# A three-layer graph attention kernel: places of DVE's checks, chain and statistics, and the load of x in two parts

## The reference

```python
def gat_layer(x, src, dst, W, a_src, a_dst, b, n_nodes):
    h = x @ W
    e = leaky_relu((h @ a_src)[src] + (h @ a_dst)[dst], 0.2)
    m = segment_max(e, dst)
    ex = exp(e - m[dst])
    alpha = ex / segment_sum(ex, dst)[dst]
    return segment_sum(alpha[:, None] * h[src], dst) + b

h = maximum(layernorm(x), 0)
x = x + gat_layer(relu(gat_layer(h, W1 128x256)), W2 256x128)
h = maximum(layernorm(x), 0)
x = x + gat_layer(h, W 128x128)
```

## Time and profile before

| | us |
|---|---|
| median of 3 runs | 685.88 (685.61 to 686.31) |
| profiled execution | 684.96 |
| its span in the trace | 683.1 |
| DVE busy | 639.8 (94%) |
| PE busy | 591.5 (87%) |
| ACT busy | 484.3 (71%) |
| POOL busy | 460.1 (67%) |
| mean granted clock of PE, as a share of full | 0.963 |

### The profile page before, as it was taken

One profiled execution on the slowest core, in us unless ns is written; L12 is line 12 of the kernel. 1 busy time (PEld: TensorE's weight loads), 2 busy tenths in 40 slices (PEclk: granted clock), 3 DMA queues, 4 the chain that ended last, 5 costly groups with the idle time before them and its releaser, 6 DMA issues.

```text
span 683.1 us, 13824 instructions
## 1 busy us (share of the span) xinstructions
PE 591.5 (87%) x5571; PEld 573.1 (84%) x5571; DVE 639.8 (94%) x911; ACT 484.3 (71%) x719; POOL 460.1 (67%) x448
## 2 busy tenths in 40 slices
PE   1729865899978999999999899999989989999994
PEld 1628755789878999899989799999988979999994
DVE  3999999999999989999987998999998899999993
ACT  0416544656969688887666788989886698888891
POOL 5579101889928565775954675858598678697883
PEclk9978986899999999999999999999999999999999
DMA  2410002000000000000100100000010010110001
GB/s 70 119 56 2 1 7 6 35 2 1 20 1 1 20 1 20 2 1 8 26 14 1 27 1 20 2 19 1 8 20 20 1 27 6 35 32 8 20 1 42
DMA packets 22325, 12.07 MB, mean 18 GB/s; under 512 B 12393, under 2 KB 20055, under 8 KB 22255
## 3 DMA queue, kind: packets, MB, share of 16 engines
q1 hardware_dynamic: 21455, 9.85, 6.3%
q0 software_dynamic: 800, 1.26, 0.6%
HBM read 9.47 MB, written 1.64 MB: 16 GB/s over the span
## 4 chain that ended last, share of the span: by engine, by line
DVE 51%; PE 29%; issue 8%; DMA 5%; POOL 4%; ACT 2%; POOLq 0%; DVEq 0%
PE ps L1813 21%; DVE scratch L951 20%; DVE ps L1067 15%; DVE scratch L1149 5%; DMA xr<-in_x 3%; POOL scratch L751 2%; DVE ps L1069 2%; DVE ps L1079 1%; PE ps L1866 1%; PE ps L1821 1%; PE ps L1844 1%; DVE scratch L1067 1%; DMA gathered<-in_edges,start_i 1%; DVE gathered L1149 1%; PE ps L1780 1%
## 5 line engine op out<-in xcount | busy, mean ns | idle before, releaser
L1813 PE MATMUL ps<-hB,scratch 125*125 125x129 f32 x3450 | 404.5, 276 | 21.1 <-DVE scratch L1149 17.6
L1813 PEld LDWEIGHTS ps<-hB,scratch 125*125 125x125 f32 x3450 | 390.9, 189 | 28.4 <-DVE scratch L1149 22.6
L751 POOL TENSOR_TENSOR scratch<-scratch,C 125x625 f32<-125x625 f32 x239 | 304.3, 1285 | 113.0 <-ACT scratch L1569 110.9
L1067 DVE SCALAR_TENSOR_TENSOR ps<-C,a_unit,ps 125x625 f32<-125x625 fp8e3 x330 | 275.4, 866 | 2.3
L1567 ACT ACTIVATE scratch<-gathered,r_neg 125x625 f32<-125x625 f32 x219 | 176.6, 806 | 20.3 <-PE ps L1813 19.2
L1569 ACT ACTIVATE scratch<-scratch,r_src 125x625 f32<-125x625 f32 x219 | 178.9, 817 | 7.1
L1452 ACT ACTIVATE C<-ps 125x1000 fp8e3<-125x1000 f32 x80 | 78.2, 1001 | 77.9 <-PE ps L1780 77.7
L1780 PE MATMUL ps<-scratch 128*128 128x125 bf16 x1250 | 93.4, 239 | 32.7 <-DVE scratch L951 30.7
L1780 PEld LDWEIGHTS ps<-scratch 128*128 128x128 bf16 x1250 | 85.7, 108 | 39.9 <-DVE scratch L951 37.8
L1149 DVE SCALAR_TENSOR_TENSOR scratch<-ps,r_src,C 125x625 f32<-125x625 f32 x121 | 104.1, 860 | 5.4 <-PE ps L1803 5.3
L951 DVE TENSOR_TENSOR scratch<-key_lo,ps 128x4096 bf16<-128x4096 bf16 (+3 forms) x41 | 89.3, 2178 | 0.0
(11 more groups left out here) (195 smaller groups left out, 444.6 us busy)
## 6 DMA issues: line engine op xcount, KB each, us to landing
gathered<-g_lines SPq DMA_DIRECT2D x15, 305.2 KB
xr<-in_x SPq DMA_DIRECT2D x1, 1562.5 KB
out<-xr SPq DMA_DIRECT2D x4, 312.5 KB
edge_sb<-in_edges SPq DMA_DIRECT2D x1, 805.7 KB
gathered<-ext_lines SPq DMA_DIRECT2D x5, 122.1 KB
w<-in_W SPq DMA_DIRECT2D x2, 128.0 KB
out<-xr SPq DMA_DIRECT2D x1, 187.5 KB
out<-xr SPq DMA_DIRECT2D x1, 125.0 KB
```

The costliest lines, as they stand in the source:

```text
L751: g.tensor_tensor(slot[s], slot[s], C5[:, q % NC, s, :], ALU.mult).then_inc(pool_done, 1)
L1067: v.scalar_tensor_tensor(dest, counts, unit[:, s:s + 1], top, ALU.min, ALU.max).then_inc(S.top_done, 1)
L1813: last = mm(ps[0:P, acc_at(t):acc_at(t) + HW], A[:, P * t:P * (t + 1)], feat, start=opens and t in (0, 3), stop=closes, skip_group_check=True)
```

## The change

It has three parts. First, SP loads the first 12 tiles of x (`X_FIRST`) directly behind `sample_i`, ahead of the weights, and the other 13 where the whole was loaded; DVE makes the statistics of the 12 ahead of `first_keys`, and those of the 13 where it made all. (One count of the semaphore `ln_lin` more is waited for in `aggregate`.) Second, the table: in chunk 1 the transposes go from s = 14 to 16 and what hangs on them one or two steps on; in chunks 6 to 9 the chain goes from steps 2 to 3 to 4 to 5, `kappa` from 4 to 5, z from 4 to 6, the aggregates from 9 to 10. Third, the check in chunks 6 and 11 goes from s = 2 to s = 17 (`MODE_AT`).

```diff
--- before.py
+++ after.py
@@ -366,6 +366,7 @@
         OWN = ((), (15, 18, 20, 22), (1, 4, 7, 10, 13, 15, 18, 20, 22), (1, 5, 9, 13, 16, 19, 22), (0, 2, 4, 7, 10, 12, 14, 16, 18, 20, 22))
 
         KEYS_TILE = 4
+        X_FIRST = 12
         FEAT_AT = tuple(KEYS_TILE + 2 + r for r in range(len(FEATS)))
         EXT_AT = FEAT_AT[-1] + 3
         OVER_AT = EXT_AT + 2
@@ -387,6 +388,7 @@
         ODD = tuple(range(3, T, 2))
         MORE = (0, 6, 12, 18, 22)
         TURN_MORE = (20, 22)
+        MODE_AT = 17
 
 
         At = namedtuple("At", "tops chain kappa z stats pool pe act rest_pe rest_act")
@@ -394,14 +396,14 @@
                    At(1, (3, 4, 5, 6), 6, (8, 9, 10), (13, 14), (14, 19), (18, None, 21), (16, 20, 23), None, None),
                    At(1, (3, 4, 5, 6), 6, (8, 9, 10), None, (14, 17, 20), (None,) * 3, (None,) * 3, None, None))
         FIRST_LAYER = (None,
-                       At(14, (15, 15, 16, 16), 16, (17, 17, 18), None, (23,), (21, 23, 27), (23, 25, 29), 25, 27),
+                       At(16, (17, 17, 18, 18), 18, (19, 19, 20), None, (24,), (23, 25, 29), (25, 27, 31), 27, 29),
                        At(10, (11, 11, 12, 12), 12, (13, 13, 14), None, (20,), (17, 20, 25), (19, 22, 27), 22, 24),
                        At(4, (5, 5, 6, 6), 6, (7, 7, 8), None, (16,), (13, 16, 22), (15, 18, 24), 19, 21))
         USUAL = (At(1, (3, 4, 5, 6), 6, (8, 9, 10), None, (14,), (12, 15, 21), (14, 17, 23), 18, 20),
-                 At(1, (2, 2, 3, 3), 4, (4, 4, 4), (9, 9), (11, 15), (15, None, 17), (14, 16, 19), None, None),
+                 At(1, (4, 4, 4, 5), 5, (6, 6, 6), (10, 10), (11, 15), (15, None, 17), (14, 16, 19), None, None),
                  At(1, (3, 4, 5, 6), 6, (8, 9, 10), None, (14, 17, 20), (None,) * 3, (None,) * 3, None, None))
         BEFORE_LAST = (At(1, (3, 4, 5, 6), 6, (8, 9, 10), None, (14,), (12, 14, 19), (13, 16, 21), 17, 18),
-                       At(1, (2, 2, 3, 3), 4, (4, 4, 4), (9, 9), (11, 15), (15, None, 17), (14, 16, 19), None, None))
+                       At(1, (4, 4, 4, 5), 5, (6, 6, 6), (10, 10), (11, 15), (15, None, 17), (14, 16, 19), None, None))
         TURN = (At(None, (1, 1, 2, 2), 3, (3, 3, 3), None, (11,), (7, 9, 13), (9, 12, 15), 11, 13),
                 At(None, (1, 1, 2, 2), 3, (3, 3, 3), (8, 8), (11, 15), (13, None, 15), (13, 14, 16), None, None))
         EXPS = {(0, 0): 1, (1, 0): 2, (1, EARLY_TILES): 3, (1, LATE): 4, (2, 0): 5, (2, EARLY_TILES): 6, (2, LATE): 7}
@@ -496,6 +498,7 @@
         @block.sync
         def _(sp):
             sp.dma_start(sample_i[:, :], apart[0, :, :]).then_inc(edges_in, 16)
+            sp.dma_start(xr[:, 0:X_FIRST, :], x_v[:, 0:X_FIRST, :]).then_inc(x_in, 16)
             sp.dma_start(w1[:, :], W1).then_inc(weights_in, 16)
             sp.dma_start(w2[:, :, 0:D], W2.rearrange("(k p) f -> p k f", p=128)).then_inc(weights_in, 16)
             sp.dma_start(w3[:, 0:D], W3).then_inc(weights_in, 16)
@@ -510,9 +513,10 @@
             sp.dma_start(b2r[:, :], b2.unsqueeze(0).broadcast_to([P, D])).then_inc(weights_in, 16)
             sp.dma_start(b3r[:, :], b3.unsqueeze(0).broadcast_to([P, D])).then_inc(weights_in, 16)
             sp.wait_ge(first_in, 16)
-            sp.dma_start(xr[:, :, :], x_v).then_inc(x_in, 16)
+            sp.wait_ge(x_in, 16)
+            sp.dma_start(xr[:, X_FIRST:T, :], x_v[:, X_FIRST:T, :]).then_inc(x_in, 16)
             sp.wait_ge(gather_in, 16 * (WG - 1))
-            sp.wait_ge(x_in, 16)
+            sp.wait_ge(x_in, 32)
             sp.dma_start(edge_sb[:, :, :], edges.rearrange("(p k) c -> p k c", p=P)).then_inc(edges_in, 16)
             sp.wait_ge(edges_in, 32)
 
@@ -896,14 +900,23 @@
             v.memset(hA[:, :, D:HW], 1.0).then_inc(h_ones, 1)
 
             def node_statistics():
+                dve.wait_ge(x_in, 32)
+                for t in range(X_FIRST, T):
+                    last = v.bn_stats(bn6[:, t, :], xr[:, t, :])
+                last.then_inc(F.ln_lin, 1)
+                dve.wait_ge(F.ln_lin, 2)
+                for t in range(X_FIRST, T):
+                    last = v.bn_aggr(mv[:, t, :], bn6[:, t, :])
+                last.then_inc(F.ln_stats, 1)
+
+            def first_statistics():
                 dve.wait_ge(x_in, 16)
-                for t in range(T):
+                for t in range(X_FIRST):
                     last = v.bn_stats(bn6[:, t, :], xr[:, t, :])
                 last.then_inc(F.ln_lin, 1)
                 dve.wait_ge(F.ln_lin, 1)
-                for t in range(T):
-                    last = v.bn_aggr(mv[:, t, :], bn6[:, t, :])
-                last.then_inc(F.ln_stats, 1)
+                for t in range(X_FIRST):
+                    v.bn_aggr(mv[:, t, :], bn6[:, t, :])
 
             def first_keys():
                 hi, lo, dl, ok, src, dst = (plane[:, 0, :] for plane in (k_hi, k_lo, k_dl, k_ok, src_i, dst_i))
@@ -933,6 +946,7 @@
             dve.wait_ge(iota_ready, 1)
             v.tensor_copy(ps[:, IOTA:IOTA + COLS * LANES // 2],
                           hB[:, 0:COLS * LANES // 2]).then_inc(iota_copied, 1)
+            first_statistics()
             dve.wait_ge(first_in, 16)
             first_keys()
             dve.wait_ge(iota_copied, 1)
@@ -1134,7 +1148,7 @@
                 last.then_inc(S.ln_lin, 1)
 
             def aggregate(S, q):
-                dve.wait_ge(S.ln_lin, q % NC + 2)
+                dve.wait_ge(S.ln_lin, q % NC + (3 if S is F else 2))
                 for t in range(CT):
                     last = v.bn_aggr(mvc[:, t, :], bn6c[:, t, :])
                 last.then_inc(S.ln_stats, 1)
@@ -1206,7 +1220,7 @@
                             extremes_late(L)
                         if s == LATE:
                             negative_r(L, LATE, T)
-                    if L and c == 1 and s == 2:
+                    if L and c == 1 and s == MODE_AT:
                         over_nodes(2 * L, ext_all, all_ready)
                         set_mode(L)
                 if q < len(FIRST_TOPS):
```

## The result

| | median us | runs |
|---|---|---|
| before | 685.57 | 684.93 to 686.31 (8) |
| changed | 688.67 | 687.60 to 690.03 (8) |

What follows compares the result with a forecast made beforehand. DVE was taken to set the pace in the count stage, DVE and PE side by side in later windows. Terms -1.67 + 2.5 - 1.2 - 0.4 + 1.55 = +0.8 against the profiled 684.96; 686.5 us written, range 684.0 to 688.8.

Steps and rivals of the forecast that it cites:

- The start: Before the keys: 12 tiles' statistics fit DVE's idle time, weights behind x cost nothing, L929 held until 41.28; -1.67 us.
- Rival D: Start: x's first load delays weights or gathers, so statistics leave free time; up to +1.7, 688.2; chance 0.09 (D and E).
- L929's hold: After the second statistics: DVE's L929 is held by POOL's L676 until 41.28, gain -1.67 us; not held, -3.65.
- Chunk 1: Transposes behind two blocks at the lower clock make DVE wait and products 18, 20, 22 late; +2.5 us, all passing.
- Chunk 6: Check and chain moved: DVE's 1.19 wait for PE's rows at 418.66 goes, -1.2 us; L1020's hold taken as unchanged.
- -0.4 for 7 and 8: Chunks 7 and 8: L1079's waits of 0.22 each go, as two top steps stand ahead of it; -0.4 us.
- Chunk 9: rz comes two top steps later and passes through POOL and PE to DVE, every link already late; +1.55 us.
- Rival C: Chunks 6 to 8: POOL's late rz is not hidden, PE waits for POOL; +4.0 us, 690.5; chance 0.10.
- A: Start: rival that L929 is not held by POOL; 2.0 us less, 684.5; chance 0.17.
- B: Chunk 1: rival that the clock stays up or returns sooner, PE loses 0.6 and not 2.5; 684.6; chance 0.12.

Runs made afterwards that it cites:

- e1: Only the start changed against the kernel before: x in two parts, 12 tiles' statistics ahead of the keys; 686.74 us, 1.0015.
- e7: Only the start changed against the kernel before, with x's first 12 tiles issued by ACT and not SP; 683.57 us, 0.9970.
- e6: Only the start changed against the kernel before, with six tiles of x, issued behind the weights; 699.78 us, 1.0210.
- e4: Only the check moved, from s = 2 to s = 17 in chunks 6 and 11, against the kernel before; 682.72 us, 0.9961.
- e14: Kernel before with the check at s = 17 and chunk 1's new row, its chain begun behind own product 18; 684.96 us, 0.9988.
- e8: Kernel before with the check at s = 17 and the later chain in chunks 6 to 8, chunk 9 as before; 683.71 us, 0.9973.
- e3: Only the table rows of chunks 6 to 9 changed against the kernel before, check left at s = 2; 686.15 us, 1.0008.
- e11: Only chunk 9's table row changed against the kernel before; 687.57 us, 1.0037.

## Why the prediction was wrong, step by step

- **The start, -1.67 forecast, about 0 found: the step that failed.** x's landing (11.3) and the length of the statistics were right. "7 us after 11.3, so I cost that at nothing" was wrong: the cover was counted from the end of x, as if the weights were there then. They are fifteen transfers behind it on the same queue, whose issue alone ended 5.7 us later, and they then landed as the gathers ran. The trace of before has no landing of the last weight, only that PE did not wait at 18.28; I took the absence of a wait for 7 us of room. An estimate from the later traces: the last weight landed at about 22.2 with its issue 5.7 us late, and at about 23.0 with 5.9 in e1, so at some 16.5 to 17.1 in the kernel before, with 1.2 to 1.8 us of room (if issue to landing took as long there). Rival D had the mechanism, but with the wrong size: I let it cost what lies in the free time (up to 1.7), when it passes to DVE in full, 3.57. e7 shows it.
- **L929's hold** never came to be tried: in no kernel did this line meet POOL's L676. That DVE's operations can last to the end of a POOL instruction is shown by e6's L926 and L930 and by L1020 (1.20 before, 0.32 in the changed kernel, 0.15 in e4). For L930 this agrees with what the Trainium skill, page "SBUF — State Buffer", section "Who interferes with whom", says of two SBUF inputs: such a DVE instruction contends with a GpSimd instruction that reads SBUF.
- **Chunk 1, +2.5 forecast, +3.0 found: right.** The clock, DVE's wait (2.4 to 2.5), product 18 (0.9) came as worked out; product 20 was 0.60 late for 0.8. 0.93 of the 3.0 stand in chunk 2, in all six kernels with a new row for chunk 1, also in e14, where chunk 1 itself lost nothing: 0.54 of it are the transposes of the features, which the row puts behind the next chunk's rows and so behind the table's mark. The other 0.4 is about what the forecast lacks; why it arises was not resolved.
- **Chunk 6, -1.2 and -0.4 for 7 and 8 forecast, -1.79 found: a term too small.** I took L1020's hold at its new place as unchanged; it fell from 1.20 to 0.32 (0.9 us). What I forecast for the chain's place was of the wrong sign: L1079's waits of 0.22 went, but waits of 0.54 for PE's rows came (452.94), as rz's delay passes through POOL and ACT to the features (this path is argued). e4 against e8: 0.8 to 1.0 us lost.
- **Chunk 9, +1.55 forecast, 1.66 and 1.63 found in e3 and e11, 2.82 in the whole: mechanism and size right, but for the clock.** The forecast had POOL's wait at 2.4 (2.35) and DVE's at 3.1 (2.96 in e3). It did not ask what PE's wait, grown from 0.93 to 3.00, does to TensorE's clock, although the same trace showed this in chunk 1.
- **Rival C**, a PE wait for POOL in chunks 6 to 8, did not come, but for one of 0.28 in chunk 8 (at 473.61; the same in e3 and e8).
- The sum: 1.7 (start) + 0.5 (chunk 1) + 1.3 (chunk 9 and its clock) - 0.2 (chunks 6 to 8) + 0.1 = 3.4 us, less 0.2 in chunks 3 to 5: 3.2 us above the forecast's +0.8 by the traces, the count stage's clock left out (5.07 - 1.07 = 4.0). By the medians it is 2.5 (3.1 for 0.6); the trace, the slowest of eight, has its clock's longer stay in chunk 9, which not every execution need have. Two slips in the forecast's own figures change nothing in this: 685.88 + 0.8 is 686.7 and not 686.5, and half of A and B with their sum make 0.20 and not 0.27 for faster.

What stays open: why TensorE's clock stays at the lower level some 3.4 us in one execution and 6.8 in another behind the same wait, why it did not fall in chunk 1 of four traces, and the 0.4 us of chunk 2. e11's time is 2.5 us above before where chunk 9 has 1.6 in its trace; the count stage's 1.2 lies beside it, and how often that comes is not known. That L929 would be held was not tried. e1's +1.0 and the changed kernel's 0.1 at the same place are two executions of a landing that varies.

## What to carry to other kernels

A large transfer that is put ahead of others on a queue can delay all of them, as here by 5.7 us: cost the latest of those behind it, and if the trace shows no wait for it, take its room as unknown, not as the distance to its first use. Where a step is moved off the path of the engine that waits, look also at how long the waiting engine has stood still: with waits of PE of some 3 us its clock fell here in most traces, and in chunk 9, where the change made such a wait, the clock's longer stay cost 1.2 us beyond it. Try parts apart: of four here, one gained 3.05 us, and the others cost 1.0, 2.9 and 0.4.

## What the runs showed of the hardware that was not expected

- Issuing the first weight's transfer on SP took 0.36 us alone, 2.06 behind six tiles of x and 5.74 to 5.93 behind twelve, while ACT's queue issued the twelve in 0.57 us (e7, from 1.23) without holding SP.
- Six tiles of x took 16 us to land when they were issued at 8.13, beside the gathers of the edges (e6); twelve issued at 1.25 took 10 us.
- Around a PE wait of 2.9 to 3.6 us, the granted clock was at 1.2 GHz for some 3.4 us in some executions and for some 6.8 in others (chunk 6: four traces each, with the same wait of 3.60 to 3.61; chunk 9: two each). The longer stay took 1.1 to 1.25 us of the kernel's time.
